# High and low parts of the values in separate operands, three products a key chunk in place of two, in the adapter stage of a three-stage kernel

## The chip, the cores and the metric

One core of a Trainium2 chip runs the whole program. The metric is the device time of one execution in microseconds; lower is better. The time before is the median of three runs.

## The reference

The input is a batch of 8 sequences of 256 tokens with 160 features, and a context of 512 rows with 96 features for each. Two layers follow each other. The first, called the adapter here, is a cross attention with 8 heads of 20 features and a small second branch:

```python
enc, ca = encoder_hidden_states[:, :508], encoder_hidden_states[:, 508:]
hs = mha(hidden @ Wq, enc @ Wk, enc @ Wv)             # 8 heads of 20 features, 508 keys
ca_q1 = einsum('btc,th->bch', ca, Wq_ca)[:, indices]  # 96 distinct rows
ca_hs1 = mha(ca_q1, residual, residual)               # keys and values are the 256 tokens
ca_hs2 = mha(ca_hs1 @ Wq, ca @ Wk_ca, ca @ Wv_ca)     # 4 keys
out = (hs + ca_hs2) @ Wout + b_out + residual
```

The second layer is a self attention, a cross attention (both 20 heads of 64 features) and a GEGLU feed forward. It is unchanged. Everything is in float32, and the kernel keeps that precision by splitting operands into a high and a low part.

## The kernel before

The program runs four stages one after the other: `adapter`, `attention` for self, `attention` for cross, and `feed_forward`. Only `adapter` is touched. It fills about the first 302 us.

In the adapter the work is cut into 32 pairs of heads (8 batches, `APAIRS` = 4 pairs each), and a loop over 39 slots runs a software pipeline: in slot g the queries and keys of pair g are projected, the row maxima of pair g-2 are found, the scores of pair g-4 are computed and exponentiated, and pair g-5 is weighed with the values. A slot has two steps. The order on each engine is written out by hand: `items(g)` lists the work of a slot, each engine walks through it in that order, and semaphores with fixed counts hold the engines together. Three shared PSUM banks go round in that order; the maxima, the scores and the weighed values have banks of their own.

What follows each other on the engines in a slot, as far as the change touches it:

- TensorE, step 0: `find_max` of step 0 (L2094, it waits until VectorE has read the maxima bank), `score` (L2106), the transposes and small products of that slot, the turned maxima (L1940), then `weigh` for groups 0 and 1. Step 1: `find_max` of step 1, `score`, the projections of queries and keys (L2085), `weigh` for groups 2 and 3, then what is left of the list, `weigh_tokens` (L2163, L2164) as the last in every fourth slot.
- VectorE: maxima of step 0 (L1882), the items of step 0, maxima of step 1, the items of step 1 (among them, in every fourth slot, L1800 to L1804, which finish what `weigh_tokens` made), and at the end of the slot L1903 to L1909, which finish the pair that `weigh` made. Then comes the next slot's L1882.
- GpSimd: the low part of the probabilities (L1613, two in a slot), of the branch's probabilities (L1622, twice in four slots), of the tokens as values (L1617), and pieces of the next stage's weights (L201).

The probabilities are float32 in `probs`; their upper 16 bits, read as bfloat16, are the high part, and `probs_l` (float16) the rest. The values are held in one tile `v` with rows of `AW` = 41 entries for each head: 20 high parts, 20 low parts and a one, all bfloat16. One matmul of 41 columns with the high probabilities and one with the low ones for each of the 4 key chunks leave both halves side by side in `pv_bank`, and the column of ones gives the sum of the probabilities. A pair has 4 groups (2 heads, 2 halves of the queries), so `weigh` issues 32 matmuls a pair. VectorE then takes the reciprocal of the sums, adds the two halves with a `reduce_sum` into the SBUF tile `whole_v`, and multiplies (L1909); `attn_ready` from L1909 lets `weigh` write the bank again. `weigh_tokens` and L1800 to L1804 do the same for the branch with the tile `xv` (8 heads, 2 token halves, 32 matmuls a batch).

Lines that the prediction names beside these: L1781 adds the stage's output to the rows of x, L1946 transposes the rows of x of a later batch, L1997 transposes the result of L1804, L1796 subtracts maxima that it reads from PSUM, and L715 is the multiplication of the self and cross attention, which reads its values from PSUM.

Of the kernel before, what the change touches and what calls it, by code (L numbers as in the profile page):

```python
# [17 lines left out]
P = 128  # L18
# [1183 lines left out]
AW = 2 * AD + 1  # L1202
# [84 lines left out]
def adapter(nc, x, x_dram, const, ident_tile, shapes, ctx_dram, l0, self_weights):  # L1287
# [90 lines left out]
    with stack:  # L1378
        def sb(what, shape, dt):
            return stack.enter_context(nc.sbuf_tensor(f"{name}_{what}", shape, dt))  # L1380
# [27 lines left out]
        v = [sb(f"v{j}", [P, KT, AH, AW], BF16) for j in two]  # L1408
# [10 lines left out]
        whole_v = sb("whole_v", [P, 4, AD], F32)  # L1419
# [16 lines left out]
        xv = sb("xv", [P, QT, AH, AW], BF16)  # L1436
# [3 lines left out]
        whole_q = sb("whole_q", [CDIM, AH, AD], F32)  # L1440
# [131 lines left out]
        def _(pool):  # L1572
# [13 lines left out]
            for j in two:  # L1586
                nc.gpsimd.memset(v[j][:, :, :, 2 * AD:AW], 1.0)
            nc.gpsimd.memset(xv[:, :, :, 2 * AD:AW], 1.0)
# [9 lines left out]
            def slot(g):  # L1598
# [16 lines left out]
                if (b := batch(g, 4)) is not None:  # L1615
                    pool.wait_ge(xv_hi, b + 1)
                    nc.gpsimd.tensor_tensor(xv[:, :, :, AD:2 * AD], tokens(b), xv[:, :, :, 0:AD], ALU.subtract).then_inc(xv_ready, 1)  # L1617
# [15 lines left out]
        def _(act):  # L1633
# [8 lines left out]
            def extra(key):  # L1642
# [19 lines left out]
                elif what == "v":  # L1662
                    rows = slice(2 * key[2], 2 * key[2] + 2)
                    nc.scalar.copy(v[j][:, rows, :, 0:AD], bank_[:, :].rearrange("p (c h d) -> p c h d", c=2, d=APAD)[:, :, :, 0:AD]).then_inc(v_hi, 1)
# [14 lines left out]
            def slot(g):  # L1679
                for step in range(ROUNDS):  # L1680
# [8 lines left out]
                    for at, key in items(g):  # L1689
# [5 lines left out]
                        elif key[0] == "xv":  # L1695
                            if key[1] > 0:
                                act.wait_ge(filled, order.filled(("qw", key[1] - 1)))
                            nc.scalar.copy(xv[:, :, :, 0:AD], tokens(key[1])).then_inc(xv_hi, 1)
# [33 lines left out]
        def _(dve):  # L1732
# [15 lines left out]
            def extra(key):  # L1748
# [18 lines left out]
                elif what == "v":  # L1767
                    dve.wait_ge(v_hi, b * 2 + key[2] + 1)
                    rows = slice(2 * key[2], 2 * key[2] + 2)
                    nc.vector.tensor_tensor(v[j][:, rows, :, AD:2 * AD], bank_[:, :].rearrange("p (c h d) -> p c h d", c=2, d=APAD)[:, :, :, 0:AD],  # L1770
                                            v[j][:, rows, :, 0:AD], ALU.subtract).then_inc(emptied, 1)
# [467 lines left out]
```

## Time and profile before

| what | value |
|---|---|
| median of 3 runs | 1356.89 us |
| lowest and highest of them | 1356.14 and 1364.06 us |
| the profiled execution | 1362.66 us |
| its span, first to last instruction | 1360.8 us |
| mean granted clock of TensorE, whole span | 0.954 |
| busy, whole span: TensorE, VectorE, ScalarE, GpSimd | 1255.5, 983.0, 781.0, 808.6 us |

The profile is of one execution, 5.8 us above the median, and 1.9 us of its time lie outside the span. Matmuls are pipelined: the record of one is much longer than the distance to the next, so the cost of a matmul in a row of equal ones is read from the starts. The granted clock is a share of 2.4 GHz; 0.50 is 1.2 GHz. Idle time of an engine that others do not wait for costs nothing.

### The profile page before, as it was taken

The numbers are of one execution on the slowest core, as the hardware profiler recorded it, in microseconds if no ns is written. First come the engines' busy times: TensorE is split into PE (matmuls) and PEld (weight loads), VectorE is DVE, ScalarE is ACT, GpSimd is POOL, SyncE is SP. The second block draws the span as 40 slices with busy tenths as digits, with TensorE's granted clock in tenths as the row PEclk, the third lists the DMA queues.
The fourth block names the chain that finished last, engine by engine and source line by source line (L and its number), as shares of the span: only waits on it lengthen the run. The fifth ranks groups of instructions, "written<-read, shape, count | busy, mean of one in ns | idle before, by whom it ended". The sixth has DMA issues, their size and how long they took to land. (4 is left out here: it accounts for less than half of the span.)

```text
span 1360.8 us, 38532 instructions
## 1 busy us (share of the span) xinstructions
PE 1255.5 (92%) x16252; PEld 1057.3 (78%) x16252; DVE 983.0 (72%) x1798; ACT 781.0 (57%) x1420; POOL 808.6 (59%) x865
## 2 busy tenths in 40 slices
PE   6989888867999999999889999999999999999598
PEld 4767666645989998999767888888888888887488
DVE  6787888845877777777557867676777777776476
ACT  3566666634656665666446656565665656554365
POOL 2577877656545554555525666565665656566555
PEclk9898998957999999999979999999999999999899
DMA  6111100002000000000010000000010000000000
GB/s 134 28 29 34 49 26 2 1 23 49 2 2 2 3 2 2 2 2 2 2 42 7 2 8 2 8 2 8 2 49 2 2 2 2 2 2 2 14 16 25
DMA packets 31988, 20.33 MB, mean 15 GB/s; under 512 B 21415, under 2 KB 30347, under 8 KB 31819
## 3 DMA queue, kind: packets, MB, share of 16 engines
q1 hardware_dynamic: 31819, 17.88, 5.2%
q8 instruction: 131, 2.15, 0.7%
q14 instruction: 38, 0.31, 0.1%
HBM read 16.56 MB, written 1.31 MB: 13 GB/s over the span
## 5 line engine op out<-in xcount | busy, mean ns | idle before, releaser
L530 POOL TENSOR_TENSOR cross_probs_l<-cross_probs 128x1024 f16<-128x1024 f32 x160 | 302.6, 1894 | 54.5 <-ACT cross_probs L614 54.5
L614 ACT ACTIVATE cross_probs<-cross_score 128x1024 f32<-128x1024 f32 x160 | 164.0, 1025 | 189.0 <-PE cross_score L844 189.0
L698 DVE TENSOR_REDUCE cross_top<-cross_max 128x2 f32<-128x1024 f32 x160 | 195.8, 1224 | 63.2 <-PE cross_max L818 63.2
L1613 POOL TENSOR_TENSOR ad_probs_l<-ad_probs 128x1024 f16<-128x1024 f32 x64 | 120.9, 1893 | 76.5 <-ACT ad_probs L1687 76.1
L530 POOL TENSOR_TENSOR self_probs_l<-self_probs 128x1024 f16<-128x1024 f32 x80 | 151.4, 1892 | 1.2 <-ACT self_probs L614 1.2
L864 PEld LDWEIGHTS cross_pv<-cross_v_h,cross_probs 128*128 128x128 bf16 x1280 | 116.4, 98 | 38.0 <-issue 26.8
L614 ACT ACTIVATE self_probs<-self_score 128x1024 f32<-128x1024 f32 x80 | 82.0, 1025 | 110.8 <-PE self_score L844 110.7
L864 PE MATMUL cross_pv<-cross_v_h,cross_probs 128*128 128x65 bf16 x1280 | 134.5, 195 | 6.1 <-POOL cross_probs_l L530 5.3
L865 PE MATMUL cross_pv<-cross_v_l,cross_probs 128*128 128x64 f16 x1280 | 133.2, 194 | 0.0
L866 PE MATMUL cross_pv<-cross_v_h,cross_probs_l 128*128 128x65 bf16 x1280 | 132.8, 193 | 0.0
L844 PE MATMUL cross_score<-cross_qk_h 64*128 64x256 f32 x640 | 120.4, 373 | 0.0
L865 PEld LDWEIGHTS cross_pv<-cross_v_l,cross_probs 128*128 128x128 bf16 x1280 | 118.1, 99 | 0.2
L866 PEld LDWEIGHTS cross_pv<-cross_v_h,cross_probs_l 128*128 128x128 f16 x1280 | 118.0, 98 | 0.0
L684 DVE TENSOR_TENSOR cross_qk_l<-cross_shared,cross_qk_h 128x256 fp32r<-128x256 f32 (+1 forms) x160 | 88.0, 554 | 32.5 <-ACT cross_qk_h L599 31.9
L698 DVE TENSOR_REDUCE self_top<-self_max 128x4 f32<-128x1024 f32 x80 | 97.7, 1222 | 17.8 <-PE self_max L823 17.7
L511 POOL CAST cross_maxima<-cross_top 128x4 bf16<-128x4 f32 x80 | 16.1, 201 | 151.5 <-DVE cross_top L698 151.5
L511 POOL CAST self_maxima<-self_top 128x4 bf16<-128x4 f32 x80 | 16.2, 202 | 137.6 <-DVE self_top L698 137.5
L1687 ACT ACTIVATE ad_probs<-ad_score 128x1024 f32<-128x1024 f32 x64 | 65.6, 1024 | 48.5 <-PE ad_score L2106 48.1
L599 ACT CAST cross_qk_h<-cross_shared 128x256 fp32r<-128x256 f32 (+1 forms) x160 | 76.1, 477 | 26.4 <-PE cross_shared L800 23.4
L844 PE MATMUL cross_score<-cross_qk_l,cross_qk_h 64*128 64x256 f32 x640 | 90.2, 278 | 0.0
L844 PE MATMUL cross_score<-cross_qk_h,cross_qk_l 64*128 64x256 f32 x640 | 90.1, 278 | 0.0
L684 DVE TENSOR_TENSOR self_qk_l<-self_shared,self_qk_h 128x512 fp32r<-128x512 f32 x80 | 55.2, 690 | 43.5 <-ACT self_qk_h L599 43.5
(436 smaller groups left out, 4649.3 us busy)
## 6 DMA issues: line engine op xcount, KB each, us to landing
ad_ctx_rows<-in_ctx SPq DMA_DIRECT2D x8, 192.0 KB, 2.8
cross_ctx_rows<-in_ctx SPq DMA_DIRECT2D x8, 192.0 KB, 2.6
sw_raw<-in_L_xattn_wq SPq DMA_DIRECT2D x2, 640.0 KB, 6.3
sw_raw<-in_L_xattn_wk SPq DMA_DIRECT2D x2, 640.0 KB, 4.3
sw_raw<-in_L_xattn_wv SPq DMA_DIRECT2D x2, 640.0 KB, 4.2
cw_raw<-in_L_xattn_wq SPq DMA_DIRECT2D x2, 640.0 KB, 5.3
lr_raw<-in_L_xattn_w_ff SPq DMA_DIRECT2D x2, 640.0 KB
out<-x_rows SPq DMA_DIRECT2D x8, 160.0 KB, 1.9
```

Source lines behind the costliest of these rows:

```text
L511: nc.gpsimd.tensor_copy(maxima[:, p % 2, :, :, 0], top[:, p % 2, :, :]).then_inc(max_hi, 1)
L530: nc.gpsimd.tensor_tensor(probs_l[:, n % PR, :, :].rearrange("p j k -> p (j k)"), whole, whole.bitcast(BF16)[:, 1::2], ALU.subtract).then_ ...
L599: nc.scalar.copy(qk_h[:, kept(parity, s), at:at + width], shared[ring.bank(kind, key)][:, 0:width]).then_inc(qk_hi, 1)
L614: nc.scalar.activation(probs[:, n % PR, :, :].rearrange("p j k -> p (j k)"), score_bank[:, :], ACT.Exp, scale=SCALE).then_inc(exped, 1)
L684: nc.vector.tensor_tensor(qk_l[:, kept(parity, s), at:at + width], shared[ring.bank(kind, key)][:, 0:width], qk_h[:, kept(parity, s), at:a ...
L698: nc.vector.reduce_max(out, scores, AX.X).then_inc(max_read, 1)
L844: mm = nc.tensor.matmul(score_bank[:, j * 512 + c * SEQ:j * 512 + (c + 1) * SEQ], ks[half, at, keys], qs[half, at, 0:SEQ], start=False, st ...
L864: nc.tensor.matmul(pv_bank[:, at:at + DV], hi, v_h[parity][:, c, head, :], start=c == 0, stop=False)
L865: nc.tensor.matmul(pv_bank[:, at:at + DH], hi, v_l[parity][:, c, head, :], start=False, stop=False)
L866: mm = nc.tensor.matmul(pv_bank[:, at:at + DV], lo, v_h[parity][:, c, head, :], start=False, stop=last)
L1613: nc.gpsimd.tensor_tensor(probs_l[:, n % PR, :, :].rearrange("p j k -> p (j k)"), whole, whole.bitcast(BF16)[:, 1::2], ALU.subtract).then_ ...
L1687: nc.scalar.activation(probs[:, n % PR, :, :].rearrange("p j k -> p (j k)"), score_bank[:, :], ACT.Exp, scale=SCALE).then_inc(exped, 1)
```

## The change

The rows of 41 become two tiles: `v_h` (bfloat16, 20 high parts and a one, `AV` = 21) and `v_l` (float16, 20 low parts). For each key chunk `weigh` issues three matmuls into the same columns of PSUM: high probabilities with `v_h` (21 columns), high probabilities with `v_l` (20 columns), low probabilities with `v_h` (21 columns). The product of the low probabilities with the low values is no longer formed. The bank then holds the whole sum, so the `reduce_sum` goes, and the multiplication reads it from PSUM. The branch gets the same with `xv_h` and `xv_l` (both 21 wide). One memset of 16 entries a partition is added at the start on GpSimd.

```diff
-AW = 2 * AD + 1
+AV = AD + 1
...
-        v = [sb(f"v{j}", [P, KT, AH, AW], BF16) for j in two]
+        v_h = [sb(f"v_h{j}", [P, KT, AH, AV], BF16) for j in two]
+        v_l = [sb(f"v_l{j}", [P, KT, AH, AD], F16) for j in two]
...
-                nc.gpsimd.memset(v[j][:, :, :, 2 * AD:AW], 1.0)
-            nc.gpsimd.memset(xv[:, :, :, 2 * AD:AW], 1.0)
+                nc.gpsimd.memset(v_h[j][:, :, :, AD:AV], 1.0)
+            nc.gpsimd.memset(xv_h[:, :, :, AD:AV], 1.0)
+            nc.gpsimd.memset(xv_l[:, :, :, AD:AV], 0.0)
...
-                    sums = bank_[0:CDIM, 0:AH * AW].rearrange("p (h d) -> p h d", d=AW)
-                    nc.vector.reciprocal(recip_q[:, :], sums[:, :, 2 * AD]).then_inc(recip_q_ready, 1)
-                    nc.vector.reduce_sum(whole_q[:, :, :], sums[:, :, 0:2 * AD].rearrange("p h (part d) -> p h d part", part=2),
-                                         AX.X).then_inc(recip_q_ready, 1)
-                    dve.wait_ge(recip_q_ready, b * 2 + 2)
-                    nc.vector.tensor_tensor(hs1[:, :].rearrange("p (h d) -> p h d", d=AD), whole_q[:, :, :],
+                    sums = bank_[0:CDIM, 0:AH * AV].rearrange("p (h d) -> p h d", d=AV)
+                    nc.vector.reciprocal(recip_q[:, :], sums[:, :, AD]).then_inc(recip_q_ready, 1)
+                    dve.wait_ge(recip_q_ready, b + 1)
+                    nc.vector.tensor_tensor(hs1[:, :].rearrange("p (h d) -> p h d", d=AD), sums[:, :, 0:AD],
                                             recip_q[:, :, None].to_broadcast([CDIM, AH, AD]), ALU.mult).then_inc(emptied, 1)
...
-                    nc.vector.reciprocal(recip[:, :], groups[:, :, 2 * AD]).then_inc(recip_ready, 1)
-                    nc.vector.reduce_sum(whole_v[:, :, :], groups[:, :, 0:2 * AD].rearrange("p g (part d) -> p g d part", part=2),
-                                         AX.X).then_inc(recip_ready, 1)
-                    dve.wait_ge(recip_ready, p * 2 + 2)
+                    nc.vector.reciprocal(recip[:, :], groups.rearrange("p (g d) -> p g d", d=AV)[:, :, AD]).then_inc(recip_ready, 1)
+                    dve.wait_ge(recip_ready, p + 1)
...
-                    nc.vector.tensor_tensor(out, whole_v[:, :, :].rearrange("p (h t) d -> p h t d", h=2),
+                    nc.vector.tensor_tensor(out, groups.rearrange("p (h t d) -> p h t d", h=2, t=QT)[:, :, :, 0:AD],
                                             recip[:, :].rearrange("p (h t) -> p h t", h=2)[:, :, :, None].to_broadcast([P, 2, QT, AD]),
                                             ALU.mult).then_inc(attn_ready, 1)
...
-                    nc.tensor.matmul(pv_bank[:, at:at + AW], hi, v[j][rows, c, head, :], start=c == 0, stop=False)
-                    mm = nc.tensor.matmul(pv_bank[:, at:at + AW], lo, v[j][rows, c, head, :], start=False, stop=c == KT - 1)
+                    nc.tensor.matmul(pv_bank[:, at:at + AV], hi, v_h[j][rows, c, head, :], start=c == 0, stop=False)
+                    nc.tensor.matmul(pv_bank[:, at:at + AD], hi, v_l[j][rows, c, head, :], start=False, stop=False)
+                    mm = nc.tensor.matmul(pv_bank[:, at:at + AV], lo, v_h[j][rows, c, head, :], start=False, stop=c == KT - 1)
...
-                    out = bank_[:, h * AW:(h + 1) * AW]
+                    n, out = 0, bank_[:, h * AV:(h + 1) * AV]
...
-                        nc.tensor.matmul(out, hi, xv[:, t, h, :], start=t == 0, stop=False)
-                        mm = nc.tensor.matmul(out, probs_ql[:, t, cols], xv[:, t, h, :], start=False, stop=t == QT - 1)
+                        for lhs, rhs in ((hi, xv_h), (hi, xv_l), (probs_ql[:, t, cols], xv_h)):
+                            mm = nc.tensor.matmul(out, lhs, rhs[:, t, h, :], start=n == 0, stop=n == 3 * QT - 1)
+                            n += 1
```

The copies on ScalarE that round the values (L1664, L1698) and the subtractions that make their low parts (L1770 on VectorE, L1617 on GpSimd) keep their counts and sizes and write to the new tiles.

## Rows read from the trace of the kernel before

**Rows 1.** The page, first line.

```profile
span 1360.8 us, 38532 instructions
```

**Rows 2.** Busy us by stretch: TensorE, its loads, VectorE, ScalarE, GpSimd; granted clock; DMA.

```profile
45.00:300.00 255.00, 215.93 (x2369) 169.10 (x2367) 203.09 (x394) 154.43 (x293) 180.11 (x106) 0.87 0.07 20
...
206.00:239.00 33.00, 28.60 (x311) 22.16 (x307) 27.62 (x54) 21.15 (x41) 24.14 (x14) 0.90 0.01 2
239.00:268.00 29.00, 25.39 (x304) 19.66 (x303) 25.83 (x53) 19.04 (x38) 19.57 (x12) 1.00 0.00 1
```

**Rows 3.** Waits of TensorE, 45 to 303 us: total us, times, longest us.

```profile
PE ad_shared L1946 <- DVE x_rows L1781: 9.2, 5, 2.7
PE ad_max L2094 <- DVE ad_maxima L1882: 7.3, 15, 0.6
...
PE ad_shared L1997 <- DVE ad_hs L1804: 3.8, 4, 1.3
```

**Rows 4.** Groups by line on VectorE, 45 to 303 us.

```profile
L1909 DVE TENSOR_TENSOR ad_attn<-ad_whole_v,ad_recip 128x80 f32<-128x80 f32 x32 | 18.9, 592 | 1.1
...
L1904 DVE TENSOR_REDUCE ad_whole_v<-ad_pv 128x80 f32<-128x160 f32 x32 | 9.3, 290 | 0.0
...
L1804 DVE TENSOR_TENSOR ad_hs<-ad_whole_q,ad_recip_q 96x160 f32<-96x160 f32 x8 | 6.4, 804 | 0.3
...
L1781 DVE TENSOR_TENSOR x_rows<-ad_shared,x_rows 128x160 f32<-128x160 f32 x16 | 4.6, 314 | 4.4 <-PE ad_shared L1981 4.4
...
L1796 DVE TENSOR_TENSOR ad_s<-ad_shared,ad_top 96x32 f32<-96x32 f32 x8 | 1.5, 187 | 0.3
```

**Rows 5.** Timeline of VectorE, 198 to 203 us: start us, us, line, what.

```profile
198.34 0.20 DVE L1800 RECIPROCAL ad_recip_q<-ad_shared 96x8 f32<-96x8 f32 x1
...
198.94 0.32 DVE L1804 TENSOR_TENSOR ad_hs<-ad_whole_q,ad_recip_q 96x160 f32<-96x160 f32 x1
199.18 0.17 DVE L1903 RECIPROCAL ad_recip<-ad_pv 128x4 f32<-128x4 f32 x1
...
199.59 0.24 DVE L1909 TENSOR_TENSOR ad_attn<-ad_whole_v,ad_recip 128x80 f32<-128x80 f32 x1
199.75 1.21 DVE L1882 TENSOR_REDUCE ad_maxima<-ad_max 128x2 f32<-128x1016 f32 x1
```

**Rows 6.** Timeline of VectorE, 212 to 215.6 us.

```profile
213.28 1.06 DVE L1909 TENSOR_TENSOR ad_attn<-ad_whole_v,ad_recip 128x80 f32<-128x80 f32 x1
```

**Rows 7.** Timeline of GpSimd, the same stretch.

```profile
212.77 1.47 POOL L1622 TENSOR_TENSOR ad_probs_ql<-ad_probs_q 128x768 f16<-128x768 f32 x1
```

**Rows 8.** The views of lines L1909 and L715: ns min/median/max.

```profile
L1909 DVE TENSOR_TENSOR ad_attn<-ad_whole_v,ad_recip x32: 241/445/1468, 55.8 to 295.3; 128x80 f32<-128x80 f32 x32
...
L715 DVE TENSOR_TENSOR self_attn<-self_pv,self_recip x80: 424/424/426, 340.4 to 675.8; 128x256 f32<-128x256 f32 x80
```

**Rows 9.** Timeline of TensorE, 199.98 to 201.02 us.

```profile
199.98 0.18 PE L2125 MATMUL ad_pv<-ad_v,ad_probs 128*128 128x41 bf16 x1
...
200.36 0.18 PE L2126 MATMUL ad_pv<-ad_v,ad_probs_l 124*128 124x41 bf16 x1
201.02 0.50 PE L2094 MATMUL ad_max<-ad_k_s,ad_q_s 64*128 64x508 f32 x2 [0.48 <-DVE ad_maxima L1882]
```

**Rows 10.** Timeline of TensorE, a cross attention block of 24 matmuls.

```profile
800.39 0.19 PE L864 MATMUL cross_pv<-cross_v_h,cross_probs 128*128 128x65 bf16 x1
...
801.08 0.19 PE L866 MATMUL cross_pv<-cross_v_h,cross_probs_l 128*128 128x65 bf16 x1
```

**Rows 11.** Timeline of TensorE, 16 matmuls near the end of the adapter stage.

```profile
294.06 0.21 PE L2125 MATMUL ad_pv<-ad_v,ad_probs 128*128 128x41 bf16 x1
...
294.58 0.20 PE L2126 MATMUL ad_pv<-ad_v,ad_probs_l 124*128 124x41 bf16 x1
```

**Rows 12.** Timeline of TensorE, one row.

```profile
224.45 0.30 PE L1946 MATMUL ad_shared<-shape_consts,x_rows 128*128 128x128 f32 x1 [1.77 <-DVE x_rows L1781]
```

**Rows 13.** Busy time of a low-clock stretch; columns as in group 2.

```profile
226.00:228.00 2.00, 2.00 (x10) 1.69 (x7) 1.87 (x4) 1.40 (x2) 0.76 (x2) 0.50 0.03 8
```

More of the change, by code:

```diff
@@ L1418, in adapter @@
         recip = sb("recip", [P, 4], F32)
-        whole_v = sb("whole_v", [P, 4, AD], F32)
         attn_th = sb("attn_th", [P, SEQ], BF16)
@@ L1435, in adapter @@
         top_q = sb("top_q", [CDIM, P], F32)
-        xv = sb("xv", [P, QT, AH, AW], BF16)
+        xv_h = sb("xv_h", [P, QT, AH, AV], BF16)
+        xv_l = sb("xv_l", [P, QT, AH, AV], F16)
         probs_q = sb("probs_q", [P, QT, WIDE], F32)
@@ L1439, in adapter @@
         recip_q = sb("recip_q", [CDIM, AH], F32)
-        whole_q = sb("whole_q", [CDIM, AH, AD], F32)
         hs1 = sb("hs1", [CDIM, HID], F32)
@@ L1616, in slot @@
                     pool.wait_ge(xv_hi, b + 1)
-                    nc.gpsimd.tensor_tensor(xv[:, :, :, AD:2 * AD], tokens(b), xv[:, :, :, 0:AD], ALU.subtract).then_inc(xv_ready, 1)
+                    nc.gpsimd.tensor_tensor(xv_l[:, :, :, 0:AD], tokens(b), xv_h[:, :, :, 0:AD], ALU.subtract).then_inc(xv_ready, 1)
                 for t in range(QT):
@@ L1663, in extra @@
                     rows = slice(2 * key[2], 2 * key[2] + 2)
-                    nc.scalar.copy(v[j][:, rows, :, 0:AD], bank_[:, :].rearrange("p (c h d) -> p c h d", c=2, d=APAD)[:, :, :, 0:AD]).then_inc(v_hi, 1)
+                    nc.scalar.copy(v_h[j][:, rows, :, 0:AD], bank_[:, :].rearrange("p (c h d) -> p c h d", c=2, d=APAD)[:, :, :, 0:AD]).then_inc(v_hi, 1)
                 elif what == "ot":
@@ L1697, in slot @@
                                 act.wait_ge(filled, order.filled(("qw", key[1] - 1)))
-                            nc.scalar.copy(xv[:, :, :, 0:AD], tokens(key[1])).then_inc(xv_hi, 1)
+                            nc.scalar.copy(xv_h[:, :, :, 0:AD], tokens(key[1])).then_inc(xv_hi, 1)
                         elif key[0] == "qs":
@@ L1769, in extra @@
                     rows = slice(2 * key[2], 2 * key[2] + 2)
-                    nc.vector.tensor_tensor(v[j][:, rows, :, AD:2 * AD], bank_[:, :].rearrange("p (c h d) -> p c h d", c=2, d=APAD)[:, :, :, 0:AD],
-                                            v[j][:, rows, :, 0:AD], ALU.subtract).then_inc(emptied, 1)
+                    nc.vector.tensor_tensor(v_l[j][:, rows, :, :], bank_[:, :].rearrange("p (c h d) -> p c h d", c=2, d=APAD)[:, :, :, 0:AD],
+                                            v_h[j][:, rows, :, 0:AD], ALU.subtract).then_inc(emptied, 1)
                 elif what == "ot":
@@ L1901, in slot @@
                     dve.wait_ge(pv_done, p + 1)
-                    groups = pv_bank[:, 0:4 * AW].rearrange("p (g d) -> p g d", d=AW)
-                    nc.vector.reciprocal(recip[:, :], groups[:, :, 2 * AD]).then_inc(recip_ready, 1)
-                    nc.vector.reduce_sum(whole_v[:, :, :], groups[:, :, 0:2 * AD].rearrange("p g (part d) -> p g d part", part=2),
-                                         AX.X).then_inc(recip_ready, 1)
-                    dve.wait_ge(recip_ready, p * 2 + 2)
+                    groups = pv_bank[:, 0:4 * AV]
+                    nc.vector.reciprocal(recip[:, :], groups.rearrange("p (g d) -> p g d", d=AV)[:, :, AD]).then_inc(recip_ready, 1)
+                    dve.wait_ge(recip_ready, p + 1)
                     head = p % APAIRS * 2
                     out = attn[p // APAIRS % 2][:, :, head * AD:(head + 2) * AD].rearrange("p t (h d) -> p h t d", h=2)
-                    nc.vector.tensor_tensor(out, whole_v[:, :, :].rearrange("p (h t) d -> p h t d", h=2),
+                    nc.vector.tensor_tensor(out, groups.rearrange("p (h t d) -> p h t d", h=2, t=QT)[:, :, :, 0:AD],
                                             recip[:, :].rearrange("p (h t) -> p h t", h=2)[:, :, :, None].to_broadcast([P, 2, QT, AD]),
@@ L2118, in weigh @@
                         pe.wait_ge(emptied, order.read(("v", b, 1)))
-                head, at = p % APAIRS * 2 + h, group * AW
+                head, at = p % APAIRS * 2 + h, group * AV
                 for c in range(KT):
```

## The prediction

> **What bounds the kernel now.** I read the first line of the page for the span [rows 1], then the busy time by stretch to see where the adapter stage stands [rows 2], then the waits, and last the timelines of single slots. Only the adapter stage is edited and the next stage starts when it is over, so what it gains or loses is gained or lost by the program.
>
> The reader should see first that no engine is full there: between 45 and 300 us TensorE is busy for 215.9 of 255 us, VectorE for 203.1, GpSimd for 180.1, at a mean granted clock of 0.87 [rows 2]. A chain runs through several engines. The waits of TensorE say through which: it waits for VectorE, for the rows of x (9.2 us), for the maxima bank (7.3 us, 15 times) and for the branch's result (3.8 us) [rows 3]. In a slot that I take as the pattern, VectorE does L1903, L1904 and L1909 without a gap, the next slot's maxima start on their heels at 199.75 and last 1.21 us [rows 5], and TensorE, done with its first weigh block, stands idle for 0.48 us until that reduction has read the bank, and then starts the second `find_max` at 201.02 [rows 9]. So the chain of a slot is: second `find_max`, projections, ScalarE's copies, VectorE's subtractions and its other items, L1903 to L1909, maxima of step 0, second `find_max`. The end of the pair on VectorE lies in it; the weigh blocks on TensorE mostly do not, they stand beside it with little to spare.
>
> **What the change removes from VectorE.** First the reduction: from the start of L1903 to that of L1909 it is 199.59 - 199.18 = 0.41 us [rows 5]. Afterwards L1909 waits for the reciprocal alone, 0.17 us, and the hand-over of a result within the engine, for which I take the 0.03 us left there (0.41 less the reduction, 0.290 [rows 4], and less the 0.09 by which it starts behind the reciprocal). That is 0.20, a gain of 0.21 us, and 6.7 us for 32 pairs. The branch's L1800 to L1804 take 198.94 - 198.34 = 0.60 us [rows 5] and come to 0.20 + 0.04 = 0.24: a gain of 0.36 us, 2.9 us for 8 batches.
>
> Second, a stretch of L1909 itself that has nothing to do with its size. All 32 have the same shape, but they take 241 to 1468 ns [rows 8], 592 in the mean [rows 4]. The one at 213.28 takes 1.06 us and ends at 214.34, 0.1 us after GpSimd's L1622, which ends at 212.77 + 1.47 = 214.24 [rows 6, 7]. It reads both inputs from SBUF, as GpSimd does. L715, the same multiplication with its values read from PSUM, takes 424 to 426 ns in all 80 cases, beside as much GpSimd work [rows 8]. After the change L1909 is like L715. For its length with 80 elements from PSUM I draw a line between L1796 (32 elements, 187 ns) and L1781 (160 elements, 314 ns) [rows 4]: 235 ns, nearly the undisturbed 241. So the stretch goes, 592 - 241 = 351 ns, 11.2 us in all. L1804 has a mean of 804 ns and comes to about 314 (160 elements, as L1781) [rows 4]: 3.9 us for 8.
>
> The Trainium skill has this as a rule ("SBUF — State Buffer", section "Who interferes with whom"): a VectorE instruction with two SBUF inputs contends with a GpSimd instruction that reads SBUF, one with at most one SBUF input outside the two-port modes does not. By that rule the 15.1 us of stretch go completely; if instead L1909 were stretched whatever its source, they would stay. The trace agrees with the rule, by the 424 to 426 ns of L715.
>
> VectorE is thus relieved by 6.7 + 2.9 + 11.2 + 3.9 = 24.7 us. At least nothing of it arrives, at most all of it.
>
> **What it adds to TensorE.** A pair takes 48 matmuls in place of 32, a batch of the branch 48 in place of 32: 32 x 16 + 8 x 16 = 640 more, each with a weight load. At the full clock 16 matmuls of 41 columns start from 199.98 to 200.36, 0.38 / 15 = 25.3 ns apart [rows 9]. 24 of 65 and 64 columns start 0.69 / 23 = 30.0 ns apart [rows 10]. No row has 20 columns. The upper bound is that narrower ones come no faster: 640 x 25.3 = 16.2 us more. The lower one extends the line, (30.0 - 25.3) / 24 = 0.20 ns a column, to 21 columns: 21.4 ns, 1920 x 21.4 - 1280 x 25.3 = 8.7 us more. At 1.2 GHz the 41 columns start 0.52 / 15 = 34.7 ns apart [rows 11], the half width would allow about 26, and 48 of these cost little more than 32 of those (1.25 for 1.11 us), so the low clock asks for no wider bound. I take 25.3, the row that is nearest in width. The skill says the same from its own measurements ("TensorE: Matmul & The Clock Gate", "Wait — 56ns, not 53.3ns?"): the starts of two matmuls come no closer than about 25 ns, however few the columns. By it the cost is the 16.2 us, by the line 8.7.
>
> Edits with one answer: the copies and subtractions that fill `v_h`, `v_l`, `xv_h`, `xv_l` keep their sizes; the extra memset runs in GpSimd's idle time before the first slot; no DMA and no wait is added, and the counts of the waits only follow the missing reduction. `weigh` still waits for `attn_ready`, which now comes earlier.
>
> **How much arrives, slot by slot.** Four slots make a batch. At 25.3 ns each weigh block of 24 takes 0.20 us more than one of 16.
> (a) The slot whose L1909 is followed by the transposes of the result: it had 1.06 us [rows 6], so the gain is 0.21 + 0.82. TensorE takes the transposes and then the longer block before its second `find_max`, minus 0.2: 0.8 us.
> (b) The slot after it, where L1909 is stretched in some batches (by about 0.4 us in the mean, what is left of the 11.2 us beside a), and where x is finished: TensorE waited 1.77 us for L1781 there [rows 12], behind L1909 and the maxima. 0.6 less the 0.2 of the block that follows the transposes of x: 0.45 us.
> (c) The slot with the branch's end. VectorE gains 0.21 + 0.36 + about 0.5, but TensorE has `weigh_tokens` (0.4 us more) and the weigh block (0.2 us more) in the same stretch, and its idle time before the second `find_max` was 0.48 [rows 9]. TensorE becomes the last to come here; I count 0.2 us.
> (d) The slot without any of it: 0.21 + 0.1, the block of 0.2 hides in the 0.48: 0.3 us.
> That is 1.75 us a batch and 14 us for 8. 10.7 of the 24.7 are lost to TensorE, which takes VectorE's place as the last in c.
>
> **The clock.** After a wait as in b the granted clock falls to 0.50, that is 1.2 GHz, while TensorE is busy for the whole 2.00 us [rows 13]; between 239 and 268 us, where no x is waited for, it stays at 1.00, and 29 us hold 304 matmul records where the 33 us before hold 311 [rows 2]. The change shortens the waits in a and b and puts work in between. I count 2 us of gain for it, between -3 and +8.
>
> **The sum.** Against the profiled execution: 1362.7 - 14 - 2 = 1346.7 us, its span 1344.8 in place of 1360.8 [rows 1]. The median stands 5.8 us below the profiled one, so 1356.9 - 16 = 1340.9; I say 1341.
>
> **Rivals.**
> 1. TensorE sets the pace (slower). If in every slot TensorE is the last at the second `find_max` and at the projections, the 16.2 us stand in the chain and VectorE's relief only makes its idle time longer: 1357 + 16 = 1373 us. The place is the weigh blocks; it decides from the point at which a block grows by more than the 0.48 us of [rows 9], or where low clocks have used that up. For it: the 215.9 of 255 us busy. Against: the block grows by 0.20, and TensorE's waits are for VectorE [rows 3]. Chance 0.11.
> 2. It arrives but is mostly given back. VectorE's relief moves the wait to ScalarE's copies and the projections, and in a and b only half is left: 5 to 8 us gain, 1350 us. Chance 0.19.
> 3. All of it arrives and the clock stays up: 1356.9 - 24.7 - 5 = 1327 us. It needs the line of 21.4 ns or better, so that the blocks hide. Chance 0.12.
> 4. The change doesn't do what it says: L1909 from PSUM is stretched all the same. Then 15.1 us are out of the sum, and what arrives of the 9.6 left is less than TensorE's load: about 1357. Chance 0.03.
> The forecast, 1331 to 1352 us, has 0.55.
>
> **How the numbers follow.** 1% of 1356.9, 13.6 us, is about what a measurement of this kernel tells from no change; faster by more is below 1343.3. Faster: 0.41 of the forecast's 0.55 and all of rival 3, 0.53. Within 1%: the rest of the forecast, rivals 2 and 4, 0.36. Slower: 0.11. The range goes from 1327 (rival 3) to 1357 (rivals 2 and 4) and leaves out rival 1 and the ends.
>
> **What would show it.** In the changed kernel L1909 takes 225 to 250 ns in all 32 cases and L1804 about 315 in 8 (if they vary, rival 4). From L1903 to L1909 it is 0.20 us. The matmuls of `weigh` start 25 ns apart at the full clock (21: cost of 8.7). TensorE waits less often for the maxima at the second `find_max`; if these waits are gone everywhere, rival 1 is near. L1613 on GpSimd stays at 1.89 us. The mean clock from 45 to 300 us is at or above 0.87. Wrong would make it above all a clock that falls more often, or a chain in c that costs more than the 0.2 us leave.

## The result, and the profile after

The changed kernel takes 1350.39 us (median of 11 runs) beside 1362.49 us for the kernel before, a ratio of 0.9924 with a 95% interval of 0.9896 to 0.9951 (the ratio is not simply that of the two medians, which are 12.1 us apart). By the ratio it is 10.4 us faster, where 16 were forecast. The forecast started from 1356.89 us, the median of the first three runs before; the median of all 11 is 5.6 us higher. Timed again two times later, the changed kernel came to 0.9897 and 0.9900. The mean of the three is 0.9907, 12.7 us. Three executions that lie more than 1.5% above the fastest of their kernel (1365.79 and 2243.82 us of the changed one, 1903.36 of the one with its sums in PSUM) are left out of the ratios.

First the page of the changed kernel: span, busy time, and the clock in 40 slices.

```profile
span 1347.7 us, 39773 instructions
...
PE 1262.0 (94%) x16892; PEld 1070.1 (79%) x16892; DVE 959.9 (71%) x1758; ACT 779.3 (58%) x1420; POOL 807.9 (60%) x866
...
PEclk8699999858999999999979999999999999999799
```

There are 640 matmuls more, as counted, and 40 VectorE instructions less. The span is 13.1 us shorter than that of [rows 1]. The groups of VectorE for this kernel, 45 to 296 us, answer to [rows 4]; the columns are busy us, mean ns and idle time before.

```profile
L1906 DVE TENSOR_TENSOR ad_attn<-ad_pv,ad_recip 128x80 f32<-128x80 f32 x32 | 7.7, 241 | 1.1
...
L1803 DVE TENSOR_TENSOR ad_hs<-ad_shared,ad_recip_q 96x160 f32<-96x160 f32 x8 | 2.6, 321 | 0.3
```

L1906 is the old L1909, L1803 the old L1804. The first fell from 592 to 241 ns, the second from 804 to 321. Their own views show that no case is stretched any more, against the 241 to 1468 ns of [rows 8]. Another multiplication reads both operands from SBUF and is not part of the change, that of the branch's second attention (`ad_p2n`, L1817, the old L1818). Its mean went from 336 to 538 ns over 8 cases, so 1.6 us came back there.

```profile
L1906 DVE TENSOR_TENSOR ad_attn<-ad_pv,ad_recip x32: 240/242/243, 59.9 to 282.3; 128x80 f32<-128x80 f32 x32
...
L1803 DVE TENSOR_TENSOR ad_hs<-ad_shared,ad_recip_q x8: 321/321/322, 69.1 to 275.1; 96x160 f32<-96x160 f32 x8
```

A block of 24 matmuls on TensorE, which answers to [rows 9]:

```profile
198.84 0.17 PE L2122 MATMUL ad_pv<-ad_v_h,ad_probs 128*128 128x21 bf16 x1
...
199.42 0.17 PE L2124 MATMUL ad_pv<-ad_v_h,ad_probs_l 124*128 124x21 bf16 x1
199.75 0.50 PE L2091 MATMUL ad_max<-ad_k_s,ad_q_s 64*128 64x508 f32 x2 [0.16 <-DVE ad_maxima L1881]
```

The starts are 0.58 / 23 = 25.2 ns apart: half the columns, the same distance. The idle time ahead of the second `find_max` is 0.16 us in place of 0.48. TensorE's waits, 45 to 296 us (total us, times, longest), answer to [rows 3]:

```profile
PE ad_shared L1943 <- DVE x_rows L1782: 6.0, 5, 1.2
...
PE ad_max L2091 <- DVE ad_maxima L1881: 1.2, 6, 0.3
```

The wait for the maxima is down from 7.3 to 1.2 us, that for the rows of x from 9.2 to 6.0, and that for the branch's result is gone. Below, "steady part" is the stretch from the first to the 28th start of L1903 (L1902 in the changed kernel), between the filling and the emptying of the pipeline; the second line is the rest up to the last start. A slot is counted from one such start to the next, 31 in all. Columns: start:end, us, busy time of TensorE, its loads, VectorE, ScalarE, GpSimd, granted clock, then DMA share and GB/s. Before:

```profile
55.35:271.68 216.33, 185.64 (x2050) 145.08 (x2049) 183.23 (x352) 138.05 (x263) 157.41 (x93) 0.91 0.09 23
271.68:294.82 23.14, 17.78 (x222) 14.05 (x222) 12.32 (x29) 11.16 (x20) 17.55 (x11) 0.62 0.01 1
```

After:

```profile
59.70:259.52 199.82, 184.88 (x2595) 151.55 (x2594) 165.21 (x318) 137.03 (x263) 157.40 (x93) 0.97 0.09 26
259.52:282.10 22.58, 19.21 (x302) 15.46 (x300) 7.51 (x25) 10.90 (x19) 17.27 (x11) 0.54 0.01 1
```

The steady part lost 16.5 us, at a clock of 0.97 for 0.91. Its start lies 4.3 us later. From 25 to 50 us this execution had a granted clock of 0.51, in a part that the change hardly touches, and the kernel before had 1.00. That explains at most 1.2 us of the 4.3: in two later profiles of the changed kernel the clock there is 1.00, and the first L1902 starts at 58.55 and 58.51. In the other kernels it starts at 57.0 to 59.0, so the 55.35 of the profile before was early; why is not known.

### The profile page after: what moved, and what is told of

Read it like the earlier page. It is cut to its first block and busy times, and to the rows that moved or that the text cites. A ratio compares the mean times of both kernels' runs of the same rounds, so it can differ in the third digit from the quotient of the medians.

```text
span 1347.7 us, 39773 instructions
## 1 busy us (share of the span) xinstructions
PE 1262.0 (94%) x16892; PEld 1070.1 (79%) x16892; DVE 959.9 (71%) x1758; ACT 779.3 (58%) x1420; POOL 807.9 (60%) x866
## 5 line engine op out<-in xcount | busy, mean ns | idle before, releaser
L698 DVE TENSOR_REDUCE cross_top<-cross_max 128x2 f32<-128x1024 f32 x160 | 195.6, 1223 | 63.6 <-PE cross_max L818 63.6
```

The costliest lines, as they stand in the source:

```text
L698: nc.vector.reduce_max(out, scores, AX.X).then_inc(max_read, 1)
```

## Experiments

Ratios are to the kernel before on the same chip, with 95% intervals; 0.001 is 1.36 us. A "Theory" or "Rival" with a letter is one of the explanations named in the expectation above it or in an earlier one. The experiments are told in the order of the questions.

**Is it the multiplication's second SBUF operand?** Only the place of the sum changes, in the kernel before, and the multiplication reads it there (the cut lines):

```diff
+                    whole = pv_bank[:, 256:256 + 4 * AD].rearrange("p (g d) -> p g d", d=AD)
-                    nc.vector.reduce_sum(whole_v[:, :, :], groups[:, :, 0:2 * AD]...
+                    nc.vector.reduce_sum(whole, groups[:, :, 0:2 * AD]...
...
+                    whole = bank_[0:CDIM, 336:336 + AH * AD].rearrange("p (h d) -> p h d", d=AD)
-                    nc.vector.reduce_sum(whole_q[:, :, :], sums[:, :, 0:2 * AD]...
+                    nc.vector.reduce_sum(whole, sums[:, :, 0:2 * AD]...
```

> The kernel before with one edit: reduce_sum leaves its sums in free columns of the same PSUM bank, so that both multiplications read one operand from PSUM. The number and length of all other instructions stay. If the stretch of the multiplications is contention between two SBUF reads and GpSimd, L1909's successor takes 240 to 250 ns in all 32 cases (mean 592 before) and the branch's about 320 (804); if it is something else, they vary as before. Theory A: 15.1 us of stretch go at no cost to TensorE, and 8 to 12 us arrive (ratio 0.991 to 0.994), as much as the whole change brings. Rival B: 0 to 4 us arrive.

Measured: 0.9851 (0.9819 to 0.9883), 1344.77 us. The views of its two multiplications:

```profile
L1911 DVE TENSOR_TENSOR ad_attn<-ad_pv,ad_recip x32: 240/241/242, 58.9 to 276.4; 128x80 f32<-128x80 f32 x32
...
L1805 DVE TENSOR_TENSOR ad_hs<-ad_shared,ad_recip_q x8: 320/320/321, 66.7 to 269.0; 96x160 f32<-96x160 f32 x8
```

The stretch is gone with nothing else touched, and the reduction itself keeps its length (300 ns for 290). So it was the second operand in SBUF, as the rule in the prediction has it. But 20.3 us arrive, more than the 8 to 12 expected and more than the 15.1 us that the stretches themselves last. This kernel also beats the changed one. It was timed twice more.

> The kernel before with both sums in PSUM once more, so that its ratio (0.9851) can be set beside the other kernels of this call and, with two measurements each, beside the changed kernel (0.9924 and 0.9897). Theory: 0.983 to 0.988 again, 5 to 9 us faster than the changed kernel. If the first was luck of the clock: 0.990.

Measured 0.9855 (0.9814 to 0.9897).

> The kernel before with both sums in PSUM beside the changed kernel on one chip: 0.985 to 0.987. If the distance to the changed kernel in the earlier calls was that between two chips, the two are within 0.002.

Measured 0.9848 (0.9803 to 0.9893), and beside it on the same chip the changed kernel:

> The changed kernel beside the kernel before with both sums in PSUM, on one chip. From the earlier calls: 0.990 to 0.992, 5 to 9 us slower than the sums in PSUM.

Measured 0.9900 (0.9865 to 0.9934). Side by side the changed kernel is 0.0052 behind, 7 us. The intervals still overlap, but the three values of one kernel all lie above the three of the other. The first repetition of the changed kernel was

> The changed kernel as it is, beside the others on the same chip, so that its distance to them is not one between two chips. If the sum of its parts holds (relief of VectorE 20.7 us, cost of the matmuls 10 to 11 us), its ratio is 0.991 to 0.994 here too.

with 0.9897 (0.9866 to 0.9929), just below what was expected.

**Where do more than 15.1 us come from?** First the two multiplications by themselves: the first half of the diff above alone, then the second alone.

> The kernel before with the sum in PSUM for the main attention alone; the branch's multiplication still reads two SBUF operands (mean 804 ns before). The stretch of L1909 was 11.2 us, that of the branch 3.9. If the arrivals go with the sizes, three quarters of the 20 us of the run with both edits: ratio 0.987 to 0.990. If the slot in which x is finished decides (its wait is behind L1909), nearly all of it: 0.985 to 0.987.

Measured 0.9924 (0.9893 to 0.9954), less than either case expected.

> The kernel before with the sum in PSUM for the branch alone, the other half of the run that had it for the main attention alone (0.9924; both together 0.9851 and 0.9855). The branch's multiplication was stretched by 3.9 us in all. If the two add up, about 9 us come from it, ratio 0.992 to 0.995, more than twice its stretch, because the wait of TensorE behind it (up to 1.3 us) no longer ends in a stretch at 1.2 GHz. If it needs both, 0.997 to 1.000.

Measured 0.9933 (0.9908 to 0.9958). 10.4 and 9.1 us: the two add up to 19.5, about what both bring together, though each is known to some 4 us only. The branch's 3.9 us of stretch bring 9. The kernel before shows a way how, at 96 us. VectorE, then GpSimd, then TensorE, each by its timeline:

```profile
95.93 1.89 DVE L1804 TENSOR_TENSOR ad_hs<-ad_whole_q,ad_recip_q 96x160 f32<-96x160 f32 x1
```

```profile
94.74 2.90 POOL L201 TENSOR_TENSOR sw_wq_s<-sw_raw,sw_wq_s 64x1280 fp32r<-64x1280 f32 x1 [1.33 <-ACT sw_wq_s L195]
```

```profile
97.87 0.30 PE L1997 MATMUL ad_shared<-shape_consts,ad_hs 96*128 96x96 f32 x1 [1.34 <-DVE ad_hs L1804]
```

L1804 ends 0.18 us after GpSimd's piece of the next stage's weights, TensorE stands still for 1.34 us until this result is there, and about 2 us later the clock falls. The same kernel's busy time by stretch, columns as above:

```profile
96.00:98.00 2.00, 0.66 (x5) 0.41 (x6) 2.00 (x3) 1.49 (x2) 1.92 (x2) 1.00 0.02 4
98.00:100.00 2.00, 1.18 (x22) 0.86 (x22) 1.97 (x4) 0.99 (x4) 2.00 (x2) 0.91 0.68 136
100.00:102.00 2.00, 2.00 (x10) 1.68 (x11) 1.61 (x2) 0.89 (x1) 0.42 (x1) 0.50 1.02 281
...
106.00:108.00 2.00, 2.00 (x10) 1.46 (x10) 1.15 (x6) 0.65 (x2) 0.00 (x0) 0.50 0.24 92
```

The slots after it then take 9.78 and 8.60 us (from one L1903 to the next) where the kernel with its sums in PSUM takes 7.28 and 6.40. There the same work at the same place keeps its clock, and TensorE's wait is gone:

```profile
96.00:98.00 2.00, 1.93 (x27) 1.51 (x28) 1.93 (x8) 1.30 (x2) 2.00 (x1) 1.00 0.02 4
98.00:100.00 2.00, 1.53 (x21) 1.25 (x18) 2.00 (x3) 1.58 (x6) 1.92 (x3) 1.00 0.34 75
100.00:102.00 2.00, 1.91 (x25) 1.36 (x24) 1.49 (x3) 1.35 (x3) 2.00 (x2) 1.00 0.98 212
```

The run with the sum in PSUM for the main attention alone shows the branch's part by itself, for there only L1804 is still stretched. Its 13th and 14th slot:

```profile
149.67:159.84 10.17, 7.05 (x104) 5.51 (x101) 8.81 (x18) 6.32 (x10) 9.62 (x7) 1.00 0.06 19
159.84:168.56 8.72, 8.04 (x66) 6.41 (x66) 6.53 (x13) 3.29 (x8) 4.58 (x3) 0.66 0.20 39
```

L1804 takes 1.90 us in the 13th slot, 1.58 more than unstretched. The slot takes 10.17 us at the full clock, where 8.60 is the length with both sums in PSUM: the whole stretch arrives. The slot behind it then takes 8.72 us at 0.66 and the next 8.00 at 0.73, for 7.29 and 6.42. The 5th and 6th slot repeat it (10.26 at the full clock, 8.30 at 0.79, for 8.63 and 7.28). In this profile the two stretched multiplications thus cost 3.2 us by their length and 4.0 us by the low clock behind them, 7.2 together, most of the 9.1.

The steady part and the rest of the kernel with both sums in PSUM:

```profile
58.43:255.63 197.20, 172.27 (x2050) 134.39 (x2049) 171.52 (x353) 136.48 (x263) 157.12 (x93) 0.99 0.10 26
255.63:276.01 20.38, 14.38 (x222) 11.56 (x222) 9.55 (x30) 10.95 (x20) 17.34 (x11) 0.86 0.01 2
```

**Is it the clock by itself?** In six slots (in five of them TensorE waits for the rows of x) it gets work without use ahead of the turned maxima:

```diff
                     bank_ = claim(key)
+                    for _ in range(8 if b % 4 == 3 and b < 24 else 0):
+                        nc.tensor.matmul(bank_[:, 256:512], wq_h[:, 0:2, :]..., wq_h[:, 0:4, :]..., start=True, stop=True)
                     pe.wait_ge(max_read, (b + 1) * ROUNDS)
```

> The kernel before plus 8 matmuls of 256 columns without use (about 0.9 us at the full clock), in the six slots in which TensorE then waits for the rows of x, in place of a part of that wait. Everything else as before, the stretch too. Theory D (a part of the gain of the sum in PSUM is the granted clock, which stays up when the wait of 1.8 us is shorter): 3 to 8 us faster than the kernel before, mean clock from 60 to 280 us up from 0.91 to 0.94 or more. Rival E (the clock is a by-product, the chain runs through VectorE): no change or up to 2 us slower.

Measured 1.0008 (0.9985 to 1.0031): no change, Theory D's gain is absent, as Rival E had it. But the work did not raise the clock dependably: the mean granted clock of the whole program has a median of 0.956 over its executions, for 0.955 before, so the median does not test what a higher clock alone would bring. The profiled execution, which is among its fastest, shows it once. It has the clock that Theory D wanted and a steady part 6.0 us shorter than before:

```profile
58.83:269.12 210.29, 181.24 (x2098) 142.33 (x2097) 184.72 (x352) 137.20 (x263) 157.27 (x93) 0.98 0.09 24
```

It also tells the length of the stretches from the clock. One slot of it with both multiplications stretched:

```profile
156.75:167.53 10.78, 8.17 (x113) 6.63 (x111) 9.42 (x18) 6.44 (x10) 9.28 (x6) 1.00 0.05 16
```

It has the full clock and still lasts 10.78 us, where the sums in PSUM have 8.60: the length of this slot is the stretch. Taking for each of the 26 slots behind the first its length at the full clock (from this profile or that of the kernel before), the stretches cost about 8 us there against the sums in PSUM. The profiled kernel before lost 18 us in the same slots. By this estimate the other 10 go with its low clocks.

> The kernel before with both sums in PSUM and the same 8 matmuls without use in the six slots. Its clock is already at 0.97 from 60 to 280 us without them, so both theories expect little: Theory D up to 2 us faster than without them (ratio 0.984), rival E 0 to 3 us slower, since the wait there is now at most 1.5 us and the filler partly sticks out.

Measured 0.9876 (0.985 to 0.9902), by the ratios 3.4 us slower than without the work (mean 0.9851), at the end of what Rival E allows and not what Theory D hoped for. The intervals overlap, so no difference is shown.

**What does the reduction bring, and what does the third product cost?** Without the products with the low values (left out, the output lacks them), the rest as changed:

```diff
-                    nc.tensor.matmul(pv_bank[:, at:at + AD], hi, v_l[j][rows, c, head, :], start=False, stop=False)
...
-                        for lhs, rhs in ((hi, xv_h), (hi, xv_l), (probs_ql[:, t, cols], xv_h)):
-                            mm = nc.tensor.matmul(out, lhs, rhs[:, t, h, :], start=n == 0, stop=n == 3 * QT - 1)
+                        for lhs, rhs in ((hi, xv_h), (probs_ql[:, t, cols], xv_h)):
+                            mm = nc.tensor.matmul(out, lhs, rhs[:, t, h, :], start=n == 0, stop=n == 2 * QT - 1)
```

> VectorE's half alone: as the changed kernel, but the products with the low parts of the values are left out (the output lacks them), so there are 32 matmuls a pair as before. Theory A: the price of the added matmuls comes back, 6 to 12 us faster than the changed kernel, so 17 to 24 us under the kernel before (ratio 0.982 to 0.987). Rival B: as the changed kernel, about 10 us under the kernel before (0.992). Rival C: the clock falls more often and it is no faster than the changed kernel, or slower.

Measured 0.9848 (0.9811 to 0.9885), as Theory A had it.

> VectorE's half alone (products with the low values left out) once more, beside the sums in PSUM on the same chip: the two differ by the reduction alone. If the 0.2 us that the reduction takes from each pair arrive, 3 to 7 us faster than with the sums in PSUM, ratio 0.981 to 0.984; if the stretch was all that counted, the same 0.985.

Measured 0.9882 (0.9849 to 0.9915), slower than either case expected; the mean is 0.9865. Against the sums in PSUM (mean 0.9851) it lacks the reduction, and is not faster. Against the changed kernel (mean 0.9907) it lacks the third product, and is 5.7 us faster. The other way round, the new products with VectorE as before (the low product into columns of its own, in a loop of its own ahead of the two others):

```diff
+                    nc.tensor.matmul(pv_bank[:, at + AV:at + AV + AD], hi, v_l[j][rows, c, head, :], start=c == 0, stop=c == KT - 1)
...
+                    groups = pv_bank[:, 0:8 * AV].rearrange("p (g part d) -> p g d part", part=2, d=AV)
+                    nc.vector.reduce_sum(whole_v[:, :, :], groups[:, :, 0:AD, :], AX.X).then_inc(recip_ready, 1)
```

> TensorE's half of the change alone: three products a key chunk (48 matmuls of 20 or 21 columns a pair and a batch of the branch), but the low product lands in columns of its own, and VectorE adds and multiplies as before, from SBUF. Theory A (in the changed kernel the 640 added matmuls stand partly in the chain, 25.3 ns each, 16.2 us in all): 6 to 12 us slower than the kernel before. Rival B (the blocks are hidden, the gain is small because VectorE's relief does not arrive): within 2 us of the kernel before. Rival C (more matmuls keep the granted clock up): faster than the kernel before, mean clock from 60 to 280 us above its 0.90.

Measured 1.0082 (1.0053 to 1.0111): 11.2 us slower, in the range of Theory A. Its steady part:

```profile
58.86:285.77 226.91, 208.70 (x2593) 168.14 (x2591) 181.53 (x353) 138.35 (x262) 157.23 (x92) 0.82 0.08 23
```

The clock is 0.82: more matmuls did not keep it up, against Rival C. The 22nd to 25th slot, which have the full clock but for the last (0.96), take 29.06 us where the kernel before takes 28.51. That is 0.55 us a batch or 4.4 us for 8, so by this estimate more than half of the 11.2 us goes with the low clocks and not with matmuls standing in the chain. The next run has four products in the main attention (`lo` with `v_l` added to the changed kernel):

> The changed kernel with a fourth product a key chunk in the main attention, low probabilities with low values (64 matmuls a pair, 512 more than the changed kernel). From two to three products cost 10 us for 640 matmuls in the comparison of the runs so far. Theory A (TensorE is now among the last in most slots, each further matmul of 25 ns stands in the chain): 8 to 12 us slower than the changed kernel, ratio to the kernel before 0.998 to 1.001. Rival B (the cost of the third product was that of a few slots): 2 to 5 us slower than the changed kernel, ratio about 0.994.

Measured 0.9897 (0.9862 to 0.9932), no slower than the changed kernel. Theory A missed, and Rival B as well, which had wanted 2 to 5 us.

The profiles say why the timings of these four don't add up. In a batch without x, at the full clock, the distances between the starts of L1903 (or its successors) repeat from profile to profile within a few hundredths of a microsecond, so four slots can be compared without the clock. The table has them from VectorE's timelines, in us; slot 22 goes from the 22nd start to the 23rd, and so on. Slot 24 holds the stretched L1909 of the prediction's slot a, slot 25 the projections and the branch's end, which are the prediction's b and c (without the rows of x):

| kernel | 22 | 23 | 24 | 25 | sum |
|---|---|---|---|---|---|
| before | 7.27 | 6.40 | 7.52 | 7.32 | 28.51 |
| sums in PSUM | 7.28 | 6.40 | 6.85 | 7.32 | 27.85 |
| two products, no reduction | 7.22 | 6.17 | 6.85 | 6.73 | 26.97 |
| changed | 7.23 | 6.36 | 6.85 | 7.13 | 27.57 |
| four products | 7.25 | 6.57 | 6.85 | 7.34 | 28.01 |

The rows behind the last two columns, for the changed kernel and then for the one with two products:

```profile
234.60 0.18 DVE L1902 RECIPROCAL ad_recip<-ad_pv 128x4 f32<-128x4 f32 x1
...
241.45 0.17 DVE L1902 RECIPROCAL ad_recip<-ad_pv 128x4 f32<-128x4 f32 x1
...
248.58 0.17 DVE L1902 RECIPROCAL ad_recip<-ad_pv 128x4 f32<-128x4 f32 x1
```

```profile
226.46 0.18 DVE L1902 RECIPROCAL ad_recip<-ad_pv 128x4 f32<-128x4 f32 x1
...
233.31 0.17 DVE L1902 RECIPROCAL ad_recip<-ad_pv 128x4 f32<-128x4 f32 x1
...
240.04 0.17 DVE L1902 RECIPROCAL ad_recip<-ad_pv 128x4 f32<-128x4 f32 x1
```

At the full clock the reduction's going is worth 27.85 - 26.97 = 0.88 us a batch, the third product costs 0.60, the fourth 0.44. Slot 23 shows where: 6.17 us with two products, 6.36 with three, 6.57 with four. In the slots with x at the full clock the same kernels take 8.00, 8.60 and 8.80 us, and that with its sums in PSUM 8.60. So at the full clock the changed kernel is not behind the one with its sums in PSUM but ahead, by 0.28 us in a batch without x; the 7 us that it lacks in the timings go with its low clocks, as far as the profiles show. The mean granted clock of the whole program says the same: its median over the executions is 0.963 to 0.968 with the sums in PSUM in the three measurements and 0.952 to 0.956 for the changed kernel. The low clocks take and give: the kernel with two products spends its steady part at 0.94 and what follows at 0.50, where the sums in PSUM have 0.99 and 0.86.

```profile
58.29:253.88 195.59, 177.20 (x2049) 141.49 (x2047) 164.03 (x319) 135.89 (x262) 156.85 (x92) 0.94 0.10 26
253.88:276.99 23.11, 18.65 (x222) 14.30 (x222) 7.83 (x24) 11.55 (x21) 17.57 (x11) 0.50 0.01 1
```

195.6 against 197.2 us in the steady part, but 23.1 against 20.4 behind it: what the reduction gave is taken at the end. The four products have 199.1 us at 0.99, the changed kernel 199.8 at 0.97. Why the clock falls in one kernel's slots and not in the other's was not settled. The length of the wait ahead does not decide it: in the changed kernel TensorE waits for the rows of x five times, for 1.25, 1.23, 1.09, 1.24 and 1.25 us, and only in the slots of the first two does the clock fall (to 0.83 and 0.82 in their mean). With the sums in PSUM it waits longer, 1.45 or 1.46 us each time, and falls in one of the five.

**The branch.** The changed kernel with the branch's two products of 41 columns and its sum in PSUM (128 matmuls fewer):

> The changed kernel for the main attention, and for the branch the two products of 41 columns of before with the sum left in PSUM (no stretch, 128 matmuls fewer than the changed kernel, 0.4 us more on VectorE a batch). Theory A (in the slot of the branch's end TensorE is the last to come): 1 to 3 us faster than the changed kernel. Rival B: the same or 1 us slower, since VectorE has the reduction again.

Measured 0.9854 (0.9824 to 0.9884), 7 us faster than the mean of the changed kernel: the direction of Theory A, more than twice its size. At the full clock its slots 22 to 25 take 27.38 us for 27.57, which is 1.5 us for 8 batches and in the range of Theory A; the rest is again clock. The mirror of it, main attention with two products and the sum in PSUM, branch as changed:

> Main attention as the kernel before with its sum in PSUM, the branch as in the changed kernel (three products, no reduction): 128 matmuls more than the run with both sums in PSUM, 0.36 us less on VectorE a batch. Theory A (in the slot of the branch's end TensorE is the last to come): 1 to 4 us slower than with both sums in PSUM (0.985), so 0.986 to 0.988. Rival B: the same or faster.

Measured 0.9878 (0.9843 to 0.9913), 3.7 us slower than the mean with the sums in PSUM, within Theory A's 1 to 4. But the intervals overlap, the two medians on this chip are 0.4 us apart (1344.84 and 1344.43), and its slots 22 to 25 take 27.87 us for 27.85. A cost of the branch's third product is not shown by this run.

The fastest exact kernels are thus the kernel before with both sums in PSUM (0.9851, 0.9855, 0.9848) and the changed one with the branch's products left at two (0.9854).

## Why the prediction was right or wrong

Right in direction and in what the change does to the multiplications; wrong in where and how it arrives. 16 us were forecast, 10.4 measured at first and 12.7 in the mean of three; against the 1356.89 us from which the forecast started, the median of 1350.39 is only 6.5 lower. That it lies in the range of 1327 to 1357 is in part the width of the range. The step that failed is "How much arrives, slot by slot", above all its term a, 0.8 us in each of eight slots, 6.4 of the 14 us. It priced a chain through VectorE and TensorE alone, at a fixed clock. The runs show slots of this kind that GpSimd holds at their length, another slot in which more arrives than was entered, and, in the profiles, a part of the clock nearly as large as that of the chain.

**Slot a, the failed term.** It was to gain 0.8 us each time. At the full clock the six slots of this kind in the steady part (4, 8, 12, 16, 20, 24) gain 0, 0.11, 0.36, 0, 0 and 0.67: 0.19 in the mean. In slots 4, 16 and 20 L1909 was stretched to 1.06 us and the whole stretch went, and yet the slot is as long as before. GpSimd has a piece of the next stage's weights there (L201, 2.9 to 3.2 us) beside its own work. Slot 16 before, then slot 16 and slot 20 of the changed kernel:

```profile
180.06:187.97 7.91, 6.65 (x74) 5.01 (x74) 7.33 (x13) 6.70 (x12) 7.70 (x4) 1.00 0.30 81
```

```profile
173.29:181.19 7.90, 7.04 (x90) 5.47 (x90) 6.31 (x13) 6.68 (x12) 7.69 (x4) 1.00 0.32 88
204.49:212.40 7.91, 7.03 (x90) 5.46 (x90) 6.31 (x12) 6.70 (x12) 7.70 (x4) 1.00 0.00 0
```

VectorE is relieved of 1.0 us in slot 16 (7.33 to 6.31), and the length stays; GpSimd is busy for 7.7 us of it in both kernels. Slots 16 and 20 take 7.90 to 7.92 us at the full clock in every kernel here, with two, three or four products. That GpSimd sets the pace there is read from these lengths and busy times; no run with less work on GpSimd tested it. The prediction has no path through GpSimd. Slot 24, with the same stretch before and none of that work on GpSimd, gains nearly what was foreseen (7.52 to 6.85).

- **b and c.** They are one slot and not two, and the slot without either comes twice. They were to gain 0.65 us together. Without x that slot gains 0.19 (7.32 to 7.13). With x, at the full clock, it goes from 10.59, 8.87, 10.78, 9.79 and 8.68 us to 8.60: 1.14 in the mean. The forecast counted the stretch of L1804 at nearly nothing because "TensorE becomes the last to come here". But TensorE itself waited for L1804, 1.34 us at 97.87, its whole stretch arrived (10.17 for 8.60), and slots at a low clock followed.
- **d.** It was to hide its longer block in the 0.48 us of idle time and to gain 0.3. In a batch without x it gained 0.04 (7.27 to 7.23), and the other slot of its kind 0.04 (6.40 to 6.36). The forecast had looked only at the first weigh block of a slot. The second one, behind the projections, grows as well: 6.17, 6.36 and 6.57 us for two, three and four products.
- **The clock.** 2 us were counted, between -3 and +8. In the profiled steady part it went from 0.91 to 0.97. Summed at the full clock, the 26 slots behind the first gained about 9 us (the forecast's 1.75 a batch would be 11.4), while the profiled ones lost 16.8. So the clock has about 8 us in these two profiles, nearly half. In the timed medians its part is not known. The work without use did not raise it, so it was not had that way.
- **The stretch of L1909 and L1804.** Right in kind: both read from PSUM are never stretched, 241 and 321 ns against 235 and 314 forecast. The support from L715 was weaker than stated: GpSimd is busy for 0.56 of the time there (188.8 of 335.9 us) and 0.71 in the adapter (180.1 of 255), and [rows 8] does not show it. What the relief is worth was mis-sized: 15.1 us were entered, of which a part should arrive; alone they brought 20.
- **The reduction.** 9.6 us were entered. The start of L1906 does lie 0.20 us behind that of L1902 (228.24 and 228.44), as forecast, and at the full clock the going of the reduction is worth 0.88 us a batch, 7.0 for 8. In the timed medians none of it was found (0.9865 without it, 0.9851 with it).
- **The matmuls.** Right in their own price: 25.2 ns for 20 and 21 columns, the upper bound of 16.2 us in all. At 1.2 GHz a block of 24 starts within 0.63 us (272.78 to 273.41), 27.4 ns apart, where the forecast's estimate was about 26.
- **The rivals.** Rival 1 (TensorE sets the pace, slower) did not occur, but its mechanism has a part in the cost of the third product, 0.60 us a batch at the full clock. Rival 2, given back in part, has 1350 us, the measured median; that is luck in the number, for it gives 5 to 8 us of gain from a lower start and has the relief end at ScalarE's copies, where the runs show GpSimd, the third product and the clock. Rival 3 did not occur, and even with two products the ratio is 0.9865. Rival 4 is refuted by the 240 to 243 ns.

## What to carry to other kernels

Look at the spread of a VectorE group before its mean: the same shape between 241 and 1468 ns was a wait in disguise, and moving one of two SBUF operands to PSUM removed it here for the price of one address, with 20 us for 15.1 us of stretch. A stall on one engine can cost more than its length where TensorE waits behind it and goes on at 1.2 GHz: 3.2 us of stretch cost 7.2. Before a gain is counted in every slot, look in each for an engine without gaps: in three of six slots GpSimd was busy nearly all the time, and 0.8 us less of VectorE's stretch gained nothing. Compare slots at the full clock beside the timings, since the two put the kernels in a different order here. And split a change into its parts before paying for all of it: the operands that moved were worth more than the whole change with its third product.

## What the runs showed of the hardware

Matmuls of 20 and 21 columns with a weight load each start 25.2 ns apart at the full clock, those of 41 columns 25.3 and those of 65 and 64 columns 30.0 [rows 9, 10]. The first two are the same, so the straight line through the widths that gave 21.4 ns was wrong. That agrees with the Trainium skill ("TensorE: Matmul & The Clock Gate", "Wait — 56ns, not 53.3ns?"), which gives about 25 ns as the least distance.

The VectorE multiplication with one operand in PSUM took 240 to 243 ns in 32 of 32 cases, 17 of them wholly within the time of a GpSimd instruction, that with both in SBUF up to 1468 ns. In the kernel before, each of these multiplications of more than 0.4 us (17 of L1909, 4 of L1804) ended 0.08 to 0.18 us after a GpSimd instruction that was under way. This agrees with "SBUF — State Buffer", "Who interferes with whom", of the Trainium skill.

The kernel with the new products alone has TensorE busy for 208.7 of 226.9 us at a granted clock of 0.82, the one with its sums in PSUM for 172.3 of 197.2 us at 0.99. The first is not shown to lose its clock by its load: a matmul lasts longer at the low clock, so the busy time grows with it. What makes the clock fall in one slot and not in the like one of another kernel stays open.
